# Low products shared out tile by tile, and two products placed later in their engines' orders, in a scan and expert kernel

## The chip, the cores and the metric

The kernel runs on one core of a Trainium2 chip. The time is the device time of one launch in microseconds (us). The kernel before took 1074.97 us, the median of 3 runs (1071.48 to 1076.53).

## What is computed

The input x has 2 rows of 1024 tokens of width 512. It is normalised per token (layernorm, called xn below). Two branches read xn, and their product is added to x.

```
proj = xn @ W_in.T ; x, gate = halves of proj (1024 each)
x  = silu(conv_b + causal 4-tap convolution of x along the tokens)
ts, Bm, Cm = rms-normalised parts of x @ W_x.T     (32, 16, 16)
dt = softplus(ts @ W_dt.T + b_dt)
state[d, n] = state[d, n] * exp(dt[d] * A[d, n]) + dt[d] * x[d] * Bm[n]   over the tokens
y[d] = sum over n of state[d, n] * Cm[n]
s  = ((y + x * D) * silu(gate)) @ W_out.T
g  = silu(top-2-of-8 expert mixture of xn)          (expert: 512 x 512)
out = x_in + s * g
```

Everything is float32. The recurrence is what makes the work serial: every one of 1024 channels with 16 states each needs a scan over 1024 tokens, twice.

## The kernel before, in words

**Tiles and quads.** The tokens are cut into 4 chunks c of 512 (chunks 0 and 1 are the first row, 2 and 3 the second), the 1024 channels into 8 tiles t of 128. n = 8c + t counts the 32 tiles, and all loops of the main part run over n. A tile's 16 states per channel are laid out as 4 quads q of 4 banks of [128 x 512]; m = 4n + q counts the 128 quads. Banks 0 and 1 of a quad are its low half, banks 2 and 3 its high half.

**One quad** takes these steps, each on its own engine: ScalarE makes the decays exp(dt*A) into PSUM (`decays`, L801); GpSimd makes the drives dt*x*B in a ring of 4 buffers in SBUF (`drives`, L588), from `rep`, which a DMA broadcasts out of DRAM for every tile; VectorE scans bank after bank (`scans`, L1175); the scanned states are multiplied by C, the high half always by VectorE (`products`, L1185), the low half either by VectorE or by GpSimd (`low_products`, L601); TensorE sums the product over the states into `y_ps` (`sums`, L1426). A drive buffer is free again when the sums of the quad 4 before are done. `POOL_QUADS` names for each tile the quads whose low product GpSimd makes; for these the low scans write to SBUF instead of PSUM. There are 98 of them.

**What ends a tile.** TensorE opens the sum of a tile with the skip product diag(D) times x (`skip`, L1420), which needs the tile before to have been read out of `y_ps`: VectorE multiplies `y_ps` by the silu of the gate (`gate_tile`, L1202), once the last quad of that tile is summed.

**Expert slots.** The tokens are sorted by expert into 23 slots of 128 rows for each of the two rows of input. Up to two slots are worked off in a tile, a first and a second one: TensorE transposes the slot (`turn_slot`, L1400), ScalarE copies the transposed slot to SBUF (`copy_slot_T`, L811), TensorE multiplies it by the expert's weights (`expert`, L1411), ScalarE copies the result out. GpSimd scatters token rows to the slots (`put_rows`, L552) and gathers them again (L566, L573).

**Around it.** In a tile, TensorE also makes the gate's products (`gate_in`, L1386), the x product of a tile of the next chunk (`next_x`, L1322, an early and a late one), the step sizes of two tiles on (L1363), and in tiles 8, 9, 16, 17, 18, 24 and 25 the output products of the chunk before (`out_tile`, L1458). ScalarE takes the first tap of the convolution (L710), VectorE the other three (`convolve`, L1114). VectorE makes step sizes out of the softplus parts (`step_sizes`, L1154 to L1150).

**What sets the order.** Every engine has its own instruction queue, written out by hand in one block per engine; an engine takes its instructions strictly in that order and waits at semaphores. Nothing is planned at run time. VectorE's order in tile n is: low scans and high half of quad 0, `gate_tile(n - 1)`, low half of quad 1, an early convolution, high half of quad 1, and so on. TensorE's order is: sums of the tile before's last quad, `gate_in`, `turn_slot` of the first slot, `skip`, at some tiles an output product, `expert` of the first slot, sums of quad 0, the late x product, the second slot. GpSimd's order in tile n is drives of quad 2, low product of quad 0, drives of quad 3, low product of quad 1, drives of the next tile's quad 0, low product of quad 2, drives of the next tile's quad 1, low product of quad 3, with row stores and gathers between.

Of the kernel before, what the change touches and what calls it, by code (L numbers as in the profile page):

```python
# [17 lines left out]
PER_ROW = SEQ // TC  # L18
# [21 lines left out]
ROWS = SLOTS * P  # L40
CONSTS = 2 * P + SLOTS + RT + P + BATCH * (E + 1)

POOL_QUADS = {n: (0, 1, 2) if 6 <= n < 14 else (0, 1, 2, 3) for n in range(TILES) if 2 <= n % (PER_ROW * NT) < 14}
POOL_QUADS.update({14: (2, 3), 15: (0, 1), 16: (3,), 17: (1, 2, 3), 30: (0, 3)})
SLOT_STEPS = ({2: (0, 1), 3: (2, 3), 4: (4, 5), 5: (6, 7), 6: (8, 9), 7: (10, 11), 8: (12, None), 9: (13, 14), 10: (15, 16), 11: (17, 18), 12: (19, 20), 13: (21, 22)},
              {2: (None, 0), 3: (1, 2), 4: (3, 4), 5: (5, 6), 6: (7, 8), 7: (9, 10), 8: (11, 12), 9: (13, 14), 10: (15, 16), 11: (17, 18), 12: (19, 20), 13: (21, 22)})
CLEARS = {n: (4 * (n - 1), min(4 * n, SLOTS)) for n in range(1, 7)}
# [54 lines left out]
def scan_moe(nc, x, wx_in, wg_in, wdt_in, wxp, wring, gate_w, means, a_log, conv_w, conv_b, d_skip,  # L102
             route_consts, bc_dram, rep_rows, xn_rows, xnT_rows, slot_x, slot_rows, s_rows, out):
    with ExitStack() as ctx:
# [877 lines left out]
        def _(dve):  # L982
# [196 lines left out]
            def products(m, h):  # L1179
                n, q = divmod(m, NQ)  # L1180
                c, t = divmod(n, NT)
                dve.wait_ge(scan_ok, NR * m + 2 * h + 2)
                if t == 0:
                    dve.wait_ge(s_c[q], 16 * (c + 1))
                dve.tensor_tensor(drive[:, m % RING, 2 * h:2 * h + 2, :], sc[:, 2 * h:2 * h + 2, :],  # L1185
                                  c_all[:, q:q + 1, :].broadcast_to([P, 2, TC]),
                                  ALU.mult).then_inc(high_ok if h else low_ok, 1)

            def low(m):
                scans(m, 0)  # L1190
                if not on_pool(m):
                    products(m, 0)
# [44 lines left out]
            for n in range(TILES):  # L1237
                c, t = divmod(n, NT)
                m = NQ * n
                early, late = early_x(c, t), late_x(c, t)  # L1240
                chunk_end = t == NT - 1 and c < NCH - 1
                rms_tile = t == NT - 2 and c < NCH - 1
                even = c % PER_ROW == 0
                after_odd = c and even
                if n:
                    low(m)
                    if pe_log(n + 1):
                        times_x(n + 1)
                    scans(m, 1)
                    if chunk_end and not pe_log(n + 1):  # L1250
                        step_sizes(n + 1)
                    products(m, 1)
                if n:
                    gate_tile(n - 1)
                low(m + 1)
                if early is not None:
                    convolve(NT * (c + 1) + early)
                scans(m + 1, 1)
                if after_odd and t == 2:
                    out_tile(c - 1, 3)  # L1260
                products(m + 1, 1)
                low(m + 2)
                if after_odd and t == 1:
                    out_tile(c - 1, 0)
                high(m + 2)
                if late is not None:
                    convolve(NT * (c + 1) + late)
                if after_odd and t == 1:
                    out_tile(c - 1, 1)
                low(m + 3)  # L1270
                high(m + 3)
                if rms_tile:
                    rms(c + 1)
                elif n + 2 < TILES and not pe_log(n + 2):
                    step_sizes(n + 2)
                if after_odd and t == 1:
                    out_tile(c - 1, 2)
# [8 lines left out]
        def _(pe):  # L1286
# [116 lines left out]
            def expert(b, j):  # L1403
                if j is None:
                    return
                m = SLOTS * b + j
                loads = ((SLOTS + 1) // 2 if j % 2 == 0 else SLOTS // 2) * b + j // 2 + 1
                pe.wait_ge(s_wr[j % 2], 16 * loads)
                pe.wait_ge(xt_ev, m + 1)
                for h in range(HK):  # L1410
                    last = pe.matmul(f_ps[:, :], xT_slot[:, h, :], w_ring[:, j % 2, h, :],  # L1411
                                     start=(h == 0), stop=(h == HK - 1))
                last.then_inc(f_mm, 1)

            def skip(n):
                c, t = divmod(n, NT)
                pe.wait_ge(diag_ok, n + 1)
                if n:
                    pe.wait_ge(gated, n)
                pe.matmul(y_ps[:, :], diag[:, :], xy[:, c % 2, t, :], start=True, stop=False).then_inc(skip_mm, 1)  # L1420

            def sums(m):
                low_done(pe, m)
                pe.wait_ge(high_ok, m + 1)
                for r in range(NR):
                    last = pe.matmul(y_ps[CH * r:CH * (r + 1), :], stack[:, :], drive[:, m % RING, r, :],  # L1426
                                     start=False, stop=(m % NQ == NQ - 1))
                last.then_inc(sum_ok, 1)
# [64 lines left out]
            for n in range(TILES):  # L1493
# [12 lines left out]
                if chunk_end:  # L1506
                    add_log(n + 1)
                turn_slot(b, first_slot)
                skip(n)
                if c and even and t == 2:  # L1510
                    out_tile(c - 1, 3, HK, NT)
                expert(b, first_slot)
                sums(m)
                if rms_tile:
                    pe.wait_ge(conv_ok, NT * (c + 2))
# [106 lines left out]
```

## Time and profile before

| | value |
|---|---|
| median of 3 runs | 1074.97 us |
| profiled execution, its own time | 1074.7 us |
| its span | 1072.9 us |
| VectorE (DVE) busy | 992.7 us, 93% |
| GpSimd (POOL) busy | 919.1 us, 86% |
| TensorE (PE) busy | 855.4 us, 80% |
| ScalarE (ACT) busy | 727.6 us, 68% |
| low and high products on VectorE (L1185) | 158 at 1224 ns |
| low products on GpSimd (L601) | 98 at 2415 ns |
| drives on GpSimd (L588) | 127 at 4604 ns |

An engine's busy time is a sum over its instructions; idle time counts only where the engine's next instruction was awaited by the chain that ends last. In a timeline, a row gives the start, the duration, the instruction's line and operands, how many were merged, and in brackets how long the engine was idle before and what ended that. A duration contains a fixed part that the next instruction of the engine can overlap, so the distance of two starts is the better price. DVE is VectorE, POOL GpSimd, PE TensorE, PEld its weight loads, ACT ScalarE, SP the engine that issues most DMAs.

### The profile page before, as it was taken

The page shows a single profiled execution, that of the slowest core. Times are in us where ns is not written, and L with a number is a line of the kernel's source. Part 1 is how long each engine was busy: PE and PEld are TensorE (multiplying, and loading weights), DVE is VectorE, ACT ScalarE, POOL GpSimd, SP SyncE. Part 2 cuts the span into 40 slices and gives each one's busy share as a digit, 9 for nine tenths or more (in the row PEclk, how much of TensorE's full clock was granted, in tenths as well). Part 3 has the DMA queues.
Part 4 walks back from the last instruction along what each step waited for, and adds up shares of the span by engine and source line. Part 5 has one row for each costly group of instructions (what it writes and reads, how often), then busy time and mean ns, then how long its engine had stood idle before and what let it go on. Part 6 is the DMA issues. An engine that isn't in the chain of part 4 may idle for free.

```text
span 1072.9 us, 10237 instructions
## 1 busy us (share of the span) xinstructions
PE 855.4 (80%) x2756; PEld 316.9 (30%) x2756; DVE 992.7 (93%) x1021; ACT 727.6 (68%) x1281; POOL 919.1 (86%) x326
## 2 busy tenths in 40 slices
PE   8944467899879998898756579889898999779467
PEld 5321122333323333333211123333332333223122
DVE  6779998999999989999999888899999889999977
ACT  3657666788877766778565566688778666667533
POOL 0626898989879998888798999899988998999997
PEclk9986678999989999999877869999999999889889
DMA  9857578767688576666743842965648556664726
GB/s 335 345 159 284 225 272 326 260 238 277 245 287 313 200 265 243 227 246 228 247 129 129 235 168 108 316 216 193 230 170 317 207 206 235 226 225 167 274 39 158
DMA packets 86585, 245.93 MB, mean 229 GB/s; under 512 B 9344, under 2 KB 10752, under 8 KB 79872
## 3 DMA queue, kind: packets, MB, share of 16 engines
q1 hardware_dynamic: 67712, 197.03, 51.4%
q10 hardware_dynamic: 12672, 31.46, 7.5%
q0 software_dynamic: 6144, 16.78, 5.8%
q8 instruction: 23, 0.38, 0.1%
q14 instruction: 34, 0.28, 0.1%
HBM read 183.11 MB, written 62.13 MB: 229 GB/s over the span
## 4 chain that ended last, share of the span: by engine, by line
DVE 35%; POOL 21%; PE 17%; issue 13%; DMA 7%; ACT 6%; SPq 2%; DVEq 0%; ACTq 0%; POOLq 0%
DVE sc_ps L1175 15%; POOL drive L588 12%; DVE drive L1175 8%; POOL drive L601 6%; PE x_ps L1458 5%; DVE x_ps L1114 3%; DVE drive L1185 3%; PE y_ps L1426 2%; PE f_ps L1411 2%; DMA rep<-rep_rows 2%; PE dt_ps L1386 2%; DMA rep_rows<-dtu 2%; PE x_ps L1322 1%; ACT sc_ps L801 1%; POOL moe L573 1%
## 5 line engine op out<-in xcount | busy, mean ns | idle before, releaser
L588 POOL TENSOR_TENSOR drive<-rep,b_all 128x2048 f32<-128x2048 f32 x127 | 581.6, 4604 | 49.5 <-DMA rep<-rep_rows 41.6
L801 ACT ACTIVATE sc_ps<-rep,a_neg 128x512 f32<-128x512 f32 x512 | 331.9, 681 | 93.2 <-DVE drive L1185 61.2
L601 POOL TENSOR_TENSOR drive<-drive,c_all 128x1024 f32<-128x1024 f32 x98 | 236.7, 2415 | 18.5 <-ACT state L780 14.1
L1426 PE MATMUL y_ps<-drive,stack 128*32 128x512 f32 x1024 | 153.9, 676 | 110.6 <-POOL drive L601 64.5
L1175 DVE TENSOR_TENSOR_SCAN sc_ps<-sc_ps,state,drive 128x512 f32<-128x512 f32 x160 | 196.1, 1271 | 5.5 <-POOL drive L588 4.2
L1185 DVE TENSOR_TENSOR drive<-sc_ps,c_all 128x1024 f32<-128x1024 f32 x158 | 193.4, 1224 | 5.3
L1175 DVE TENSOR_TENSOR_SCAN sc_ps<-sc_ps,drive 128x512 f32<-128x512 f32 x156 | 181.7, 1210 | 9.9 <-ACT sc_ps L801 5.9
L1411 PE MATMUL f_ps<-w_ring,xT_slot 128*128 128x512 f32 x368 | 171.3, 609 | 15.4 <-ACT xT_slot L811 15.4
L1386 PE MATMUL dt_ps<-xnT,w_g 128*128 128x512 f32 x232 | 121.1, 670 | 28.2 <-ACT dtu L768 28.2
L1175 DVE TENSOR_TENSOR_SCAN drive<-sc_ps,state,drive 128x512 f32<-128x512 f32 x96 | 117.6, 1266 | 3.2 <-ACT sc_ps L801 3.2
L1175 DVE TENSOR_TENSOR_SCAN drive<-sc_ps,drive 128x512 f32<-128x512 f32 x100 | 116.3, 1204 | 0.3 <-POOL drive L588 0.3
L1411 PEld LDWEIGHTS f_ps<-w_ring,xT_slot 128*128 128x128 f32 x368 | 68.2, 193 | 116.8 <-issue 116.3
L1322 PE MATMUL x_ps<-xnT,w_x 128*128 128x512 f32 x192 | 89.9, 611 | 3.8 <-DMA w_x<-wx_in 3.8
L1458 PE MATMUL x_ps<-w_out,xy 128*128 128x512 f32 x176 | 82.6, 615 | 0.0
L1426 PEld LDWEIGHTS y_ps<-drive,stack 128*32 128x32 f32 x1024 | 21.4, 113 | 202.6 <-issue 116.3
L1386 PEld LDWEIGHTS dt_ps<-xnT,w_g 128*128 128x128 f32 x232 | 47.3, 215 | 109.1 <-issue 109.1
L780 ACT ACTIVATE state<-sc_ps 128x2 f32<-128x2 f32 x78 | 13.1, 168 | 58.5 <-DVE drive L1185 58.0
L1322 PEld LDWEIGHTS x_ps<-xnT,w_x 128*128 128x128 f32 x192 | 35.6, 193 | 57.5 <-issue 52.0
L1458 PEld LDWEIGHTS x_ps<-w_out,xy 128*128 128x128 f32 x176 | 32.6, 194 | 50.8 <-issue 50.2
L1363 PE MATMUL dt_ps<-dt_in,w_dt 128*128 128x512 f32 x64 | 41.3, 731 | 6.8 <-DVE dt_in L1225 5.6
L1420 PE MATMUL y_ps<-xy,diag 128*128 128x512 f32 x64 | 34.1, 615 | 14.0 <-DVE xy L1202 14.0
L768 ACT COPY dtu<-dt_ps 128x512 f32<-128x512 f32 x32 | 18.7, 585 | 36.9 <-DVE dtu L1150 36.8
(187 smaller groups left out, 1048.1 us busy)
## 6 DMA issues: line engine op xcount, KB each, us to landing
rep<-rep_rows SPq DMA_DIRECT2D x128, 512.0 KB, 6.2
w_ring<-wring SPq DMA_DIRECT2D x46, 1024.0 KB, 5.6
rep_rows<-dtu ACTq DMA_DIRECT2D x32, 512.0 KB, 2.7
x_slot<-slot_x SPq DMA_DIRECT2D x46, 256.0 KB, 6.8
slot_rows<-y_slot ACTq DMA_DIRECT2D x46, 256.0 KB, 4.3
w_g<-wg_in SPq DMA_DIRECT2D x32, 256.0 KB, 7.6
w_x<-wx_in SPq DMA_DIRECT2D x24, 256.0 KB, 3.8
slot_x<-zeros SPq DMA_DIRECT2D x1, 5888.0 KB, 20.5
```

What stands on the lines that cost most here:

```text
L588: pool.tensor_tensor(drive[:, m % RING, :, :], rep[:, n % 2, :, 1, :], b_all[:, q:q + 1, :].broadcast_to([P, NR, TC]), ALU.mult).then_inc( ...
L601: pool.tensor_tensor(drive[:, m % RING, 0:2, :], drive[:, m % RING, 0:2, :], c_all[:, q:q + 1, :].broadcast_to([P, 2, TC]), ALU.mult).then ...
L801: act.activation(sc[:, r, :], rep[:, n % 2, r, 0, :], ACT.Exp, scale=a_neg[:, lo:lo + 1]).then_inc(decay_ok, 1)
L1175: dve.tensor_tensor_scan(to, sc[:, r, :], drive[:, m % RING, r, :], state[:, lo:lo + 1] if follows else 0.0, ALU.mult, ALU.add).then_inc(s ...
L1185: dve.tensor_tensor(drive[:, m % RING, 2 * h:2 * h + 2, :], sc[:, 2 * h:2 * h + 2, :], c_all[:, q:q + 1, :].broadcast_to([P, 2, TC]), ALU. ...
L1322: last = pe.matmul(x_bank(j), w(h), xnT[:, c % 2, h, :], start=(h == 0), stop=(h == HK - 1))
L1363: pe.matmul(dt_ps[:, :], w_dt[:, t, :], dt_in[:, :], start=True, stop=True).then_inc(dt_mm, 1)
L1386: mm = pe.matmul(gate_bank(c, t)[:, :], w_g[:, h, :], xnT[:, c % 2, h, :], start=(h == 0), stop=(h == HK - 1))
L1411: last = pe.matmul(f_ps[:, :], xT_slot[:, h, :], w_ring[:, j % 2, h, :], start=(h == 0), stop=(h == HK - 1))
L1420: pe.matmul(y_ps[:, :], diag[:, :], xy[:, c % 2, t, :], start=True, stop=False).then_inc(skip_mm, 1)
L1426: last = pe.matmul(y_ps[CH * r:CH * (r + 1), :], stack[:, :], drive[:, m % RING, r, :], start=False, stop=(m % NQ == NQ - 1))
L1458: last = pe.matmul(bank, xy[:, c % 2, t, P * i:P * (i + 1)], w_out[:, t, :], start=(t == 0), stop=(t == NT - 1))
```

## The change

Three edits. The table of GpSimd's quads is changed: tile 0 gets quads 1 and 2, tile 6 gets quad 3; quad 3 of tile 16, quads 1 to 3 of tile 17, and quad 3 of tiles 18, 24 and 30 go to VectorE. VectorE's gate product of the tile before comes behind the low half of quad 1 instead of ahead of it. TensorE's skip product comes behind the first slot's expert products (and behind the output product that stands there in tile 18) instead of ahead of them.

```diff
--- before.py
+++ after.py
@@ -40,8 +40,8 @@
 ROWS = SLOTS * P
 CONSTS = 2 * P + SLOTS + RT + P + BATCH * (E + 1)
 
-POOL_QUADS = {n: (0, 1, 2) if 6 <= n < 14 else (0, 1, 2, 3) for n in range(TILES) if 2 <= n % (PER_ROW * NT) < 14}
-POOL_QUADS.update({14: (2, 3), 15: (0, 1), 16: (3,), 17: (1, 2, 3), 30: (0, 3)})
+POOL_QUADS = {n: (0, 1, 2) if 7 <= n < 14 else (0, 1, 2, 3) for n in range(TILES) if 2 <= n % (PER_ROW * NT) < 14}
+POOL_QUADS.update({0: (1, 2), 14: (2, 3), 15: (0, 1), 18: (0, 1, 2), 24: (0, 1, 2), 30: (0,)})
 SLOT_STEPS = ({2: (0, 1), 3: (2, 3), 4: (4, 5), 5: (6, 7), 6: (8, 9), 7: (10, 11), 8: (12, None), 9: (13, 14), 10: (15, 16), 11: (17, 18), 12: (19, 20), 13: (21, 22)},
               {2: (None, 0), 3: (1, 2), 4: (3, 4), 5: (5, 6), 6: (7, 8), 7: (9, 10), 8: (11, 12), 9: (13, 14), 10: (15, 16), 11: (17, 18), 12: (19, 20), 13: (21, 22)})
 CLEARS = {n: (4 * (n - 1), min(4 * n, SLOTS)) for n in range(1, 7)}
@@ -1250,9 +1250,9 @@
                     if chunk_end and not pe_log(n + 1):
                         step_sizes(n + 1)
                     products(m, 1)
+                low(m + 1)
                 if n:
                     gate_tile(n - 1)
-                low(m + 1)
                 if early is not None:
                     convolve(NT * (c + 1) + early)
                 scans(m + 1, 1)
@@ -1506,10 +1506,10 @@
                 if chunk_end:
                     add_log(n + 1)
                 turn_slot(b, first_slot)
-                skip(n)
                 if c and even and t == 2:
                     out_tile(c - 1, 3, HK, NT)
                 expert(b, first_slot)
+                skip(n)
                 sums(m)
                 if rms_tile:
                     pe.wait_ge(conv_ok, NT * (c + 2))
```

## Rows read from the trace of the kernel before

**Rows 1.** The chain that ended last, shares of the span by engine.

```profile
DVE 35%; POOL 21%; PE 17%; issue 13%; DMA 7%; ACT 6%; SPq 2%; DVEq 0%; ACTq 0%; POOLq 0%
```

**Rows 2.** VectorE's waits: us in total, times, longest.

```profile
DVE xy L1202 <- PE y_ps L1426: 11.4, 7, 4.0
...
DVE drive L1175 <- ACT sc_ps L801: 3.2, 4, 0.9
```

**Rows 3.** VectorE's timeline, tile 6, from quad 2: start us, us, instruction.

```profile
282.30 2.33 DVE L1175 TENSOR_TENSOR_SCAN drive<-sc_ps,drive 128x512 f32<-128x512 f32 x2
...
288.04 2.33 DVE L1175 TENSOR_TENSOR_SCAN sc_ps<-sc_ps,drive 128x512 f32<-128x512 f32 x2
...
295.07 0.68 DVE L1219 SCALAR_TENSOR_TENSOR dt_ps<-dt_ps,t_w 64x512 f32<-64x512 f32 x1
```

**Rows 4.** Timelines of GpSimd and VectorE, tiles 0 and 1.

```profile
101.75 9.05 POOL L588 TENSOR_TENSOR drive<-rep,b_all 128x2048 f32<-128x2048 f32 x2 [8.72 <-DMA rep<-rep_rows]
...
130.67 4.53 POOL L588 TENSOR_TENSOR drive<-rep,b_all 128x2048 f32<-128x2048 f32 x1
...
135.23 2.35 DVE L1175 TENSOR_TENSOR_SCAN sc_ps<-sc_ps,drive 128x512 f32<-128x512 f32 x2 [0.81 <-POOL drive L588]
```

**Rows 5.** Timelines of tiles 4 and 5, and a stretch of tile 4.

```profile
216.55 5.37 PE L1411 MATMUL f_ps<-w_ring,xT_slot 128*128 128x512 f32 x8 [0.36 <-ACT xT_slot L811]
...
227.26 0.78 ACT L710 ACTIVATE x_ps<-x_pad,cb,cw 128x512 f32<-128x512 f32 x1
...
228.59 1.54 DVE L1114 SCALAR_TENSOR_TENSOR x_ps<-x_pad,cw,x_ps 128x512 f32<-128x512 f32 x2
...
245.59 0.60 PE L1400 MATMUL f_ps<-ident,x_slot 128*128 128x128 f32 x4
246.03 1.02 PE L1420 MATMUL y_ps<-xy,diag 128*128 128x512 f32 x2
246.96 3.67 PE L1411 MATMUL f_ps<-w_ring,xT_slot 128*128 128x512 f32 x8
...
255.97 0.78 ACT L710 ACTIVATE x_ps<-x_pad,cb,cw 128x512 f32<-128x512 f32 x1
...
257.22 1.54 DVE L1114 SCALAR_TENSOR_TENSOR x_ps<-x_pad,cw,x_ps 128x512 f32<-128x512 f32 x2
...
core 0: us, PE busy (x) PEld busy (x) DVE busy (x) ACT busy (x) POOL busy (x), PEclk, DMA share, GB/s
...
216.50:222.00 5.50, 5.45 (x12) 2.18 (x16) 5.39 (x7) 4.69 (x8) 3.90 (x2) 0.69 0.91 311
```

**Rows 6.** Timelines of GpSimd, TensorE and VectorE, tiles 7 to 10.

```profile
316.72 2.37 POOL L601 TENSOR_TENSOR drive<-drive,c_all 128x1024 f32<-128x1024 f32 x1 [2.28 <-ACT state L780]
...
351.09 1.07 PE L1426 MATMUL y_ps<-drive,stack 128*32 128x512 f32 x8 [1.24 <-POOL drive L601]
...
406.43 1.54 DVE L1114 SCALAR_TENSOR_TENSOR x_ps<-x_pad,cw,x_ps 128x512 f32<-128x512 f32 x2 [0.91 <-ACT x_ps L710]
```

**Rows 7.** TensorE, VectorE and a DMA (from the chain), tiles 17 to 19.

```profile
635.84 1.94 PE L1426 MATMUL y_ps<-drive,stack 128*32 128x512 f32 x8 [3.72 <-POOL drive L601]
...
646.15 0.69 DVE L1208 TENSOR_TENSOR moe<-x_ps,moe 128x512 f32<-128x512 f32 x1 [3.17 <-PE x_ps L1458]
...
671.40 6.65 DMA w_x<-wx_in
...
684.42 0.69 DVE L1202 TENSOR_TENSOR xy<-y_ps,gate 128x512 f32<-128x512 f32 x1 [4.04 <-PE y_ps L1426]
...
695.67 2.35 DVE L1175 TENSOR_TENSOR_SCAN sc_ps<-sc_ps,drive 128x512 f32<-128x512 f32 x2 [0.34 <-ACT sc_ps L801]
```

**Rows 8.** GpSimd's drives from 905.3 to 1028.9, then VectorE's timeline to the end.

```profile
L588 POOL TENSOR_TENSOR drive<-rep,b_all 128x2048 f32<-128x2048 f32 x18 | 82.3, 4610 | 4.3 <-DMA rep<-rep_rows 4.2
...
1028.86 2.47 DVE L1175 TENSOR_TENSOR_SCAN sc_ps<-sc_ps,state,drive 128x512 f32<-128x512 f32 x2 [4.17 <-POOL drive L588]
...
1037.62 0.69 DVE L1202 TENSOR_TENSOR xy<-y_ps,gate 128x512 f32<-128x512 f32 x1 [1.41 <-PE y_ps L1426]
...
1064.76 2.51 DVE L1214 TENSOR_TENSOR xy<-xy,xnT 128x512 f32<-128x512 f32 x1
```

## The prediction

> **What bounds the kernel now.** I read the page's chain of waits first, then VectorE's idle time by releaser, then the timelines of VectorE, GpSimd, TensorE and ScalarE from 78 us to the end. The chain [rows 1] has no single owner: VectorE holds most of it, GpSimd and TensorE a good deal. VectorE's own waits [rows 2] are small: the gate product waited for TensorE 11.4 us in 7 places, the most that its move can return. What matters is which of VectorE's waits ends each stretch, because all else there is shifted only with it. I follow one number through the kernel: how much later (+) or earlier (-) VectorE reaches a place than before. All sums are made on the profiled execution: span 1072.9 us, time 1074.7 us, 0.3 us under the median 1074.97.
>
> **The price of one product.** With the low product on GpSimd, VectorE steps from one quad to the next in 288.04 - 282.30 = 5.74 us; with its own in 295.07 - 288.04 = 7.03 us [rows 3]. So a product costs VectorE 1.3 us; it saves GpSimd 2.3 us, a little under the 2.37 us of the product in [rows 6], since the next instruction starts just before it ends. Counted from the table, GpSimd goes from 98 to 94 products. On a VectorE that never waited the four would cost 5.2 us; what they cost here depends on each place.
>
> **Tiles 0 and 1 (quads 1 and 2 to GpSimd): +2.3 us.** GpSimd waits 8.72 us for the broadcast before the drives at 101.75 [rows 4], so quad 1's product is free. Quad 2's comes after the first of these two drives and pushes everything behind it: the second drive, 16 indirect stores in three bundles, and drives up to quad 7's at 130.67. VectorE already waited 0.81 us for that one [rows 4]. VectorE and ScalarE arrive 1.3 us sooner, but the drive lands 2.3 us later, so quad 7's scans start 2.3 us later. Behind them hang tile 3's step sizes and, behind the last stores, the slot load for tile 2, so tile 2's stalls move too. Bounds: -1.3 (the delay hidden, the sooner arrival kept) and +2.3; the nearest row is the 0.81 us wait, which leaves no room, so I take +2.3.
>
> **The skip product behind the slot's products: a gap that nothing fills.** In tile 5, TensorE ends the slot's transposes at about 246.2, runs the skip product at 246.03 and starts the expert's products at 246.96 [rows 5]: the skip product fills the time in which ScalarE copies the transposed slot. Put last, it leaves that gap open and adds 0.85 us to TensorE's queue before the quad's sums. In most tiles TensorE has slack. It lacks it where the late x product follows: in tile 5 ScalarE starts its tap at 255.97 and is through 0.5 us before VectorE's convolution at 257.22, in tile 4 it starts at 227.26 for a convolution at 228.59, slack 0.6 us [rows 5]. TensorE runs without a pause from tile 4's second slot to tile 5's, so the second delay adds to the first: 1.85 us less 0.5 of slack gives +1.4 for the two. Bounds: 0 (cover found) and +2.0. The same sums in tiles 11 to 13 and 20 and 21 stay inside 0.35 to 2 us of slack: 0.
>
> **Tile 6 (quad 3 to GpSimd): -1.3 us.** GpSimd waits again behind it before tile 7's products (the 2.28 us in [rows 6] is the last of these waits), and VectorE's steps follow without waits, also through the normalisation. Bounds: -1.3 and 0.
>
> **Tiles 7 to 10: +1.1 us.** VectorE's waits end on a chain that leaves it in tile 7: keep-state copy, GpSimd at 316.72 with its 2.28 us wait, drives and products of tile 8, TensorE at 351.09, which then never pauses until tile 10's late x product, awaited by VectorE at 406.43 [rows 6]. The gate moved behind the second quad's low scans starts this chain 0.6 us sooner, tiles 9 and 10 each add 0.85 for the uncovered skip product. -0.6 + 1.7 = +1.1; bounds -0.6 and +2.0. The gate wait of 1.0 us in tile 10 gives nothing: behind it the scans wait for ScalarE, which waits for the same output product.
>
> **Tiles 16 to 19 (quad 3 of 16, three quads of 17 and quad 3 of 18 to VectorE): -1.9 us.** Five products, 6.5 us of VectorE and 11.5 us off GpSimd. VectorE's scans of tile 17 start where the drive lands, which none of this moves. Then TensorE no longer waits 3.72 us for GpSimd's product before its sums at 635.84; the output tile follows 2.4 us sooner, and VectorE, which waited for it 3.17 us until 646.15 [rows 7], passes 2.4 us sooner in spite of three more products. From there the chain is GpSimd's residual, the weight load that landed 6.65 us after 671.40, the x product, the sums and ScalarE's tables: -2.5 us. The 4.04 us gate wait at 684.42 [rows 7] vanishes almost wholly, but VectorE then waits for ScalarE, 0.34 us before and now for 2.5 us earlier work at 695.67. So of the gate's 4 us only the chain's 2.5 remain, and tile 19's uncovered skip product takes 0.65 back. Bounds: +6.5 (no cover at all) and -4.7 (VectorE before its next wait).
>
> **Tiles 23 to 30: +0.3 us.** The tile 7 pattern again: -0.6 for the gate, +0.85 for tile 25; quad 3 of tile 24 lies in a wait of VectorE for softplus. From the broadcast of tile 27 on GpSimd has no idle time: in the stretch to quad 124 its drives show 4.3 us, all before the first [rows 8]. None of the products in that stretch leaves GpSimd before the drive for which VectorE waited 4.17 us at 1028.86, so the +0.3 arrives there whole, and VectorE's shift before it does not count.
>
> **Tile 30 and the end: -2.3 us.** Quad 3's product is gone from GpSimd right behind that drive. The gate wait of 1.41 us at 1037.62 goes [rows 8]: -1.4. GpSimd's tail of sums is 2.3 us sooner, and VectorE's first closing sum, 2.51 us at 1064.76 where its like take 0.68 [rows 8], ended only as GpSimd fell idle. So the end gains the full 2.3; bounds -2.3 and 0. The Trainium skill, SBUF — State Buffer, section "Who interferes with whom", says that a VectorE product with both inputs in SBUF and a GpSimd one block each other for a whole instruction; by that rule the long row is a lock, and the gain at the end would be 2.3 rather than 1.4 us.
>
> **Sum.** +2.3 + 1.4 - 1.3 + 1.1 - 1.9 + 0.3 - 2.3 = -0.4 us: 1074.7 - 0.4 = 1074.3 us. The moves of work return some 5.5 us and give back 5.
>
> **Rivals.** *The skip product stays covered.* If TensorE's real slack is larger than the modelled ends show, 1.4 + 1.7 + 0.65 + 0.85 = 4.6 us go: 1069.7 us; with quad 2's delay hidden as well, 3.6 more: 1066.1. For it: TensorE is busy 80% and the copy takes only 0.6 us. Against it: four of VectorE's waits already sit behind a TensorE queue with no pause.
>
> *TensorE's clock falls in the new gap (the slower side).* In the tiles where TensorE waits for the gate, it has transposes, 1.6 us idle, skip product, 0.4 us idle, expert. After the change that is one pause of over 3 us. In tile 4 the expert's products took 5.37 us at a granted clock of 0.69 for that stretch, against 3.67 in the row of tile 5 [rows 5]: 1.7 us more each, on the queue that already lacks slack. It decides where a pause of 3 us lowers the clock from 2.4 to 1.2 GHz. In four such tiles it is +6.8: 1081.1 us. Against it: the sums behind are mostly awaited by nobody at once. The Trainium skill, TensorE: Matmul & The Clock Gate, Part 1 (the HAM clock gate), says that an idle array is put back to half rate and needs activity to be released; by that rule the new pause makes this rival likelier than rows alone do, and tile 4's row agrees.
>
> *The gate's move returns its waits whole.* 11.4 less the last tile's 1.3 is 10.1 us: 1064 us. Against it: in four places the scans behind have a wait of their own for ScalarE, 3.2 us in all [rows 2], and three of these follow a gate wait. So I give it little.
>
> **How the numbers follow.** Forecast 0.50, its own range 1071.5 to 1077. Covered skip product 0.27, clock 0.18, whole gate waits 0.05. About 0.5% (5.4 us) is what a measurement tells from no change: below 1069.6 is faster, above 1080.3 slower. Forecast: nearly all of it within 0.5%, 0.04 each side. First rival: some two thirds below 1069.6. Second: seven in ten above 1080.3. Third: faster. Together faster 0.27, same 0.57, slower 0.16. The range 1067 to 1080.5 leaves out the lower end of the first and third rivals and the upper of the second.
>
> **What would show it.** Right: VectorE's products L1185 at 162 and GpSimd's L601 at 94; quad 7's scans in tile 1 near 137.5 with a wait of about 4 us for GpSimd; the skip product starting right where the expert's products end, with 0.8 us idle between transposes and expert; new short waits of VectorE for ScalarE before the late convolutions of tiles 4 and 5; waits for the gate under 3 us in sum; the wait before quad 124 still for a drive, the last VectorE sums at 0.7 us. Wrong: tile 1's scans no later than before, tiles 4 and 5 without waits, or a fall of the granted clock in tiles 4, 6, 20 and 22.

## The result: half a per cent slower

The changed kernel took 1080.27 us (median of 6 runs, 1078.08 to 1081.23), the kernel before on the same chip 1074.2 us (6 runs). The ratio is 1.0049, with a 95% interval of 1.0032 to 1.0066: 5.3 us, about 0.5%, slower. I had forecast 1074.3 us and a change within 0.5% as the likeliest case. The time lies inside my range, close to its upper edge, but the change went the other way than the sum, which had it 0.4 us faster. The mechanism that came true was one of my rivals, to which I had given 0.18.

The profiled execution took 1080.09 us, span 1078.3 us. Its chain by engine, to be held against [rows 1]:

```profile
DVE 28%; PE 28%; POOL 20%; issue 10%; DMA 7%; ACT 4%; SPq 2%; DVEq 0%; POOLq 0%; ACTq 0%
```

TensorE's share of the chain has gone from 17% to 28%, though its busy time has not grown by anything near that. VectorE's waits after, in the form of [rows 2] (us in total, times, longest):

```profile
DVE sc_ps L1175 <- ACT sc_ps L801: 11.4, 10, 2.4
DVE sc_ps L1175 <- POOL drive L588: 9.5, 3, 4.4
...
DVE drive L1175 <- ACT sc_ps L801: 7.9, 3, 2.6
DVE x_ps L1114 <- ACT x_ps L710: 5.3, 8, 1.2
...
DVE xy L1202 <- PE y_ps L1426: 1.4, 1, 1.4
```

The waits for the gate, 11.4 us before, have all but gone, as intended. But waits for ScalarE stand in their place. Before, two of these rows were:

```profile
DVE sc_ps L1175 <- ACT sc_ps L801: 7.2, 8, 2.4
...
DVE x_ps L1114 <- ACT x_ps L710: 2.0, 2, 1.1
```

The wait ahead of the scans into `sc_ps` grew from 7.2 to 11.4 us, that ahead of the scans into `drive` from 3.2 to 7.9, and eight convolutions in place of two wait for their first tap. ScalarE in turn waits for TensorE. What TensorE waits for says why; the same view, first of before, then of after:

```profile
PE f_ps L1411 <- ACT xT_slot L811: 15.4, 21, 1.2
PE y_ps L1420 <- DVE xy L1202: 14.0, 10, 2.9
```

```profile
PE f_ps L1411 <- ACT xT_slot L811: 48.4, 34, 4.3
...
PE y_ps L1420 <- DVE xy L1202: 29.6, 6, 8.8
```

L1411 is the expert product of a slot. It waited 15.4 us for ScalarE's copy of the transposed slot, never over 1.2 us; now it waits 48.4 us, up to 4.3. Tile 6 shows one such wait. TensorE's timeline (start, us), before and then after:

```profile
272.34 0.60 PE L1400 MATMUL f_ps<-ident,x_slot 128*128 128x128 f32 x4
274.55 1.10 PE L1420 MATMUL y_ps<-xy,diag 128*128 128x512 f32 x2 [1.61 <-DVE xy L1202]
276.01 3.67 PE L1411 MATMUL f_ps<-w_ring,xT_slot 128*128 128x512 f32 x8 [0.36 <-ACT xT_slot L811]
```

```profile
274.83 0.60 PE L1400 MATMUL f_ps<-ident,x_slot 128*128 128x128 f32 x4
278.50 5.37 PE L1411 MATMUL f_ps<-w_ring,xT_slot 128*128 128x512 f32 x8 [3.07 <-ACT xT_slot L811]
283.70 1.02 PE L1420 MATMUL y_ps<-xy,diag 128*128 128x512 f32 x2
284.66 1.07 PE L1426 MATMUL y_ps<-drive,stack 128*32 128x512 f32 x8
```

Transposes to expert product: 276.01 - 272.34 = 3.67 us before, 278.50 - 274.83 = 3.67 us after. The expert product does not start a moment sooner for having left the skip product's company. It waits for the copy either way, and the skip product had been running inside that wait. Now it runs behind, and the pause in front of the expert product is unbroken. Here is what the pause does (windows: stretch, length, busy time of PE, PEld, DVE, ACT, POOL, granted clock, DMA share, GB/s), before and after:

```profile
276.00:279.70 3.70, 3.69 (x12) 1.51 (x16) 3.63 (x5) 2.95 (x5) 3.70 (x2) 1.00 0.91 275
```

```profile
275.40:278.50 3.10, 0.03 (x1) 0.03 (x1) 3.10 (x4) 2.56 (x6) 3.10 (x2) 1.00 0.87 318
278.50:283.80 5.30, 5.30 (x9) 2.28 (x10) 5.19 (x8) 5.14 (x8) 4.34 (x2) 0.68 0.84 298
```

Behind a stretch with TensorE idle the granted clock is 0.68 on average, between the levels of 1.2 and 2.4 GHz, and the same eight products take 5.37 us in place of 3.67. In tiles 7 and 23 the pause is 4.34 us and the products take 5.98 and 5.93 us. The price then reaches VectorE through the second slot's transposes and ScalarE's queue:

```profile
295.24 2.35 DVE L1175 TENSOR_TENSOR_SCAN sc_ps<-sc_ps,drive 128x512 f32<-128x512 f32 x2 [2.37 <-ACT sc_ps L801]
```

Why the copy is late can be read on ScalarE's own timeline:

```profile
273.08 1.30 ACT L801 ACTIVATE sc_ps<-rep,a_neg 128x512 f32<-128x512 f32 x2
274.32 0.19 ACT L705 ACTIVATE x_pad<-halo 128x3 f32<-128x3 f32 x1
274.42 0.56 ACT L707 COPY x_pad<-x_ps 128x512 f32<-128x512 f32 x1
275.07 0.78 ACT L710 ACTIVATE x_ps<-x_pad,cb,cw 128x512 f32<-128x512 f32 x1
275.79 0.19 ACT L712 ACTIVATE halo<-x_pad 128x3 f32<-128x3 f32 x1
276.34 0.17 ACT L780 ACTIVATE state<-sc_ps 128x2 f32<-128x2 f32 x1 [0.36 <-DVE drive L1185]
276.54 1.30 ACT L801 ACTIVATE sc_ps<-rep,a_neg 128x512 f32<-128x512 f32 x2
277.78 0.57 ACT L811 COPY xT_slot<-f_ps 128x512 f32<-128x512 f32 x1
```

The transposes end at 275.43, and in its written order ScalarE has the early x block and two decays to do before the copy. The copy is late like this in tiles 4, 6, 20 and 22, which have an early x (pause 3.07 us), and in tiles 7 and 23, the last of a chunk, where ScalarE first copies the next chunk's step sizes and waits 1.2 us for VectorE to make them (4.34 us). An early x is not enough: tiles 3, 5, 19 and 21 have one too, but their pause is 0.77 us; in tile 5 ScalarE is at the copy first and waits 1.22 us for the transposes.

### The profile page after: what moved, and what is told of

It is laid out like the page before. It is cut to its first block, busy times and chain, and to the rows that moved or that the text cites. A ratio compares the mean times of both kernels' runs of the same rounds, so it can differ in the third digit from the quotient of the medians.

```text
span 1078.3 us, 10234 instructions
## 1 busy us (share of the span) xinstructions
PE 860.6 (80%) x2756; PEld 323.2 (30%) x2756; DVE 997.3 (92%) x1025; ACT 727.0 (67%) x1281; POOL 909.9 (84%) x322
## 4 chain that ended last, share of the span: by engine, by line
DVE 28%; PE 28%; POOL 20%; issue 10%; DMA 7%; ACT 4%; SPq 2%; DVEq 0%; POOLq 0%; ACTq 0%
DVE sc_ps L1175 12%; POOL drive L588 11%; PE f_ps L1411 6%; DVE drive L1175 6%; PE x_ps L1458 5%; POOL drive L601 4%; PE y_ps L1426 4%; PE x_ps L1322 3%; PE dt_ps L1386 3%; DMA rep<-rep_rows 3%; DVE drive L1185 3%; DVE x_ps L1114 2%; DMA rep_rows<-dtu 2%; POOL moe L573 2%; PE x_ps L1344 1%
## 5 line engine op out<-in xcount | busy, mean ns | idle before, releaser
L601 POOL TENSOR_TENSOR drive<-drive,c_all 128x1024 f32<-128x1024 f32 x94 | 224.4, 2388 | 16.0 <-DVE sc_ps L1175 5.8
L1411 PE MATMUL f_ps<-w_ring,xT_slot 128*128 128x512 f32 x368 | 179.6, 634 | 48.4 <-ACT xT_slot L811 48.4
L1175 DVE TENSOR_TENSOR_SCAN sc_ps<-sc_ps,state,drive 128x512 f32<-128x512 f32 x164 | 201.2, 1272 | 4.9 <-POOL drive L588 3.1
L1185 DVE TENSOR_TENSOR drive<-sc_ps,c_all 128x1024 f32<-128x1024 f32 x162 | 198.4, 1224 | 5.4
L1175 DVE TENSOR_TENSOR_SCAN sc_ps<-sc_ps,drive 128x512 f32<-128x512 f32 x160 | 186.6, 1212 | 16.5 <-ACT sc_ps L801 9.5
L1175 DVE TENSOR_TENSOR_SCAN drive<-sc_ps,state,drive 128x512 f32<-128x512 f32 x92 | 112.7, 1266 | 7.9 <-ACT sc_ps L801 7.9
L1411 PEld LDWEIGHTS f_ps<-w_ring,xT_slot 128*128 128x128 f32 x368 | 71.4, 202 | 142.1 <-issue 141.2
L1175 DVE TENSOR_TENSOR_SCAN drive<-sc_ps,drive 128x512 f32<-128x512 f32 x96 | 111.7, 1205 | 0.0
L811 ACT COPY xT_slot<-f_ps 128x512 f32<-128x512 f32 x46 | 26.6, 579 | 33.5 <-PE f_ps L1400 33.5
L1114 DVE SCALAR_TENSOR_TENSOR x_ps<-x_pad,cw,x_ps 128x512 f32<-128x512 f32 x54 | 40.7, 753 | 6.5 <-ACT x_ps L710 5.3
```

The costliest lines, as they stand in the source:

```text
L601: pool.tensor_tensor(drive[:, m % RING, 0:2, :], drive[:, m % RING, 0:2, :], c_all[:, q:q + 1, :].broadcast_to([P, 2, TC]), ALU.mult).then ...
L1114: tap = dve.scalar_tensor_tensor(out=x_bank(j) if k < K - 1 else xy[:, c % 2, t, :], in0=padded(j)[:, k:k + TC], scalar=cw[:, t * K + k:t ...
L1175: dve.tensor_tensor_scan(to, sc[:, r, :], drive[:, m % RING, r, :], state[:, lo:lo + 1] if follows else 0.0, ALU.mult, ALU.add).then_inc(s ...
```

## The experiments

The change has three parts: the **table** of products, the **gate** product behind the second quad's low scans, and the **skip** product behind the first slot's products. Runs of one group shared a chip and the runs of the kernel before; ratios are to that kernel, with 95% intervals. Microseconds "by the ratio" are differences of ratios times 1074 us. In edits the names are those of the diff.

### All combinations of the three parts

**Table alone.** The edit leaves the new `POOL_QUADS` and takes the other two parts back.

```diff
-                low(m + 1)
                 if n:
                     gate_tile(n - 1)
+                low(m + 1)
...
+                skip(n)
                 if c and even and t == 2:
                     out_tile(c - 1, 3, HK, NT)
                 expert(b, first_slot)
-                skip(n)
```

> The kernel before with the new table of c products alone; gate product and skip product at their old places. Theory 1 (TensorE's queue): what the change lost came from the skip product leaving the gap in which TensorE waits for ScalarE's copy of the first slot (3.07 us idle in tiles 6, 18 and 22, 4.34 in tiles 7 and 23, with the slot's eight products at 5.37 to 5.98 us behind it in place of 3.67), so the table alone keeps the gain of tiles 16 to 20 (the shift after - before falls from 6.33 to 1.64 us there) and pays 1.2 us in tile 0: 1069 to 1073. Theory 2 (the table): the quads of tiles 0 and 6 and the ones given back late in the table are the loss: 1078 to 1081.

Measured: 1070.67 us, ratio 0.9982 (0.9966 to 0.9998). The table is a gain, 1.9 us by the ratio, just clear of nothing. Theory 2 falls. (Where the expectation says tile 18, the pause is that of tile 20.)

**Gate and skip without the table** (old `POOL_QUADS` in the changed kernel):

```diff
-POOL_QUADS.update({0: (1, 2), 14: (2, 3), 15: (0, 1), 18: (0, 1, 2), 24: (0, 1, 2), 30: (0,)})
+POOL_QUADS.update({14: (2, 3), 15: (0, 1), 16: (3,), 17: (1, 2, 3), 30: (0, 3)})
```

and 6 in place of 7 in the table's range.

> The changed kernel with the old table: only the gate product and the skip product stand at their new places. Theory 1 (TensorE's queue): slower than the changed kernel by what the table gives, 1081 to 1086, with about 3 us idle and a slow first slot in tiles 6, 7, 22 and 23 still there. Theory 2 (the table): 1070 to 1074.

Measured: 1080.79 us, 1.0075 (1.0053 to 1.0098), just below the range of theory 1. The first slot's pause of 3.07 us stands in tiles 4, 6, 20 and 22, that of 4.34 in 7 and 23.

**Table and gate, skip product at its old place:**

```diff
+                skip(n)
                 if c and even and t == 2:
                     out_tile(c - 1, 3, HK, NT)
                 expert(b, first_slot)
-                skip(n)
```

> The changed kernel with the skip product back ahead of the first slot's products; table and gate product as changed. The skip product then waits for a gate product that stands 2.3 us later on VectorE, and the slot's products stand behind it. Theory 1a (the pair belongs together: with the late gate product the old order is as bad): 1080 to 1085, the slot's products start behind the gate product in every tile. Theory 1b (the skip product's place alone is the loss): 1069 to 1073. Theory 2 (the table): 1078 to 1081.

Measured: 1081.31 us, 1.0068 (1.0046 to 1.0091). Theory 1a: the later gate product must not have the skip product, and the expert product behind it, waiting for it.

**Table and skip, gate product at its old place:**

```diff
-                low(m + 1)
                 if n:
                     gate_tile(n - 1)
+                low(m + 1)
```

> The changed kernel with the gate product back ahead of the second quad's low scans; table and skip product as changed. Theory 1 (the skip product's place is the loss, whenever the gate product comes): 1078 to 1082, with the 3 us gap and the slow first slot of tiles 6, 7, 22 and 23 as in the changed kernel, and VectorE's waits for sums ahead of the gate product back (some 11 us in sum, a part of them in place of other waits). Rival (the late gate product holds the sums back): 1069 to 1074.

Measured: 1081.74 us, 1.0069 (1.0050 to 1.0089). VectorE's gate waits are back at 10.6 us and the time is not better: with the skip product behind, the gate's place matters little.

**Skip product alone** (the last two lines of the diff on the kernel before):

```diff
-                skip(n)
                 if c and even and t == 2:
                     out_tile(c - 1, 3, HK, NT)
                 expert(b, first_slot)
+                skip(n)
```

> The kernel before with the skip product behind the first slot's products and nothing else changed. Theory 1 (its place is the loss with either gate order): 1079 to 1084. Rival (it loses only together with the new table or the late gate product): 1072 to 1076.

Measured: 1081.75 us, 1.0072 (1.0053 to 1.0091).

**Gate product alone:**

```diff
+                low(m + 1)
                 if n:
                     gate_tile(n - 1)
-                low(m + 1)
```

> The kernel before with VectorE's gate product behind the second quad's low scans, and nothing else changed: the skip product is ahead of the slot's products still. Theory 1 (the order of TensorE's queue decides: skip product, and with it the slot's products, wait for a gate product that is 2.3 us later): 1080 to 1085. Rival (the later gate product costs only together with the new table): 1072 to 1076.

Measured: 1085.32 us, 1.0102 (1.0081 to 1.0123), the slowest of all and just above what theory 1 gave. TensorE's timeline in tile 6 of this kernel, and its windows there:

```profile
273.99 0.60 PE L1400 MATMUL f_ps<-ident,x_slot 128*128 128x128 f32 x4
278.43 2.05 PE L1420 MATMUL y_ps<-xy,diag 128*128 128x512 f32 x2 [3.84 <-DVE xy L1202]
280.27 5.32 PE L1411 MATMUL f_ps<-w_ring,xT_slot 128*128 128x512 f32 x8
```

```profile
277.00:280.00 3.00, 1.57 (x2) 0.84 (x3) 2.93 (x5) 2.72 (x5) 3.00 (x2) 0.50 0.92 299
280.20:285.50 5.30, 5.30 (x9) 1.95 (x7) 5.26 (x6) 4.69 (x8) 1.63 (x1) 0.67 1.00 364
```

The pause is 3.84 us, the skip product in it runs at a granted clock of 0.50 and takes 2.05 us, the expert product 5.32. Slow products behind a long pause are there with the other order too, so they hang on the pause, not on which product comes first.

Together, as ratios to the kernel before:

```
                  old table            new table
neither           1                    0.9982
gate              1.0102               1.0068
skip              1.0072               1.0069
gate and skip     1.0075               1.0049
```

Each way of reordering costs. With the new table both together cost least by the number, but the intervals of the three overlap. The table by itself is the only part that gains. Beside the gate product it gains too, just measurably; beside both its 0.26% is within the noise, and beside the skip product there is nothing. The change is 0.67% slower than its own table alone, 7.2 us; from the two intervals this difference is good to about 2.5 us.

### Where the 7.2 us are

How much later VectorE reaches the product `dtu` (L1150) for tile k than in the kernel before, read off its timelines, us:

```
              k=3    k=8    k=12   k=18   k=21   k=24   k=31
table alone   1.8   -0.2    0.2    1.8   -2.4   -2.4   -2.8
changed       2.6    3.7    5.2    6.3    1.6    5.4    7.4
six tiles     1.9    0.2    2.2    3.6    0.3    1.9    4.0
gap filled    2.4    0.2    1.5    2.8   -0.4    0.4    0.6
```

Against the table alone the changed kernel loses 3.1 us between k = 3 and 8 (3.9 - 0.8) and 3.8 between 21 and 24 (7.8 - 4.0). VectorE does this product one or two tiles ahead, so these are tiles 2 to 6 and 20 to 22, where the late copies are; k = 24 to 31 adds 2.4 more. These are single executions, and their level is uncertain by more than tenths: the table without tile 0's quads, an experiment further down, leaves everything up to tile 5 as in the kernel before, and still reaches k = 4 2.0 us earlier. Steps inside a row tell more than the level of a row. The last two rows are the next two experiments.

**Old order in the six tiles with a late copy** (`LATE_COPY = (4, 6, 7, 20, 22, 23)`):

```diff
+                if n in LATE_COPY:
+                    gate_tile(n - 1)
                 low(m + 1)
-                if n:
+                if n and not n in LATE_COPY:
                     gate_tile(n - 1)
...
+                if n in LATE_COPY:
+                    skip(n)
                 expert(b, first_slot)
-                skip(n)
+                if not n in LATE_COPY:
+                    skip(n)
```

(the lines of the output tile between them stand as they were)

> The changed kernel with the old order (gate product ahead of the low scans, skip product ahead of the slot's products) in the six tiles where ScalarE's copy of the first slot comes 3.07 to 4.34 us after the transposes: 4, 6, 7, 20, 22 and 23. The loss by the order was 1080.3 - 1070.7 = 9.6 us. Theory 1a (it falls in these six tiles): 1071 to 1074, no gap over 2 us ahead of a first slot, none of its eight products slower than in the kernel before, and the new waits of 2.37 us of VectorE in tiles 6 and 22 gone. Theory 1b (it is spread: 0.8 us in every tile where TensorE is what VectorE ends up waiting for): 1077 to 1080.

Measured: 1075.43 us, 1.0013 (1.0000 to 1.0026). Between the two: 0.36% or 3.9 us of the 7.2 come back; the rest, by this run, lies in the other tiles. One expectation missed: in tiles 7 and 23 the products still took 5.76 and 5.72 us, behind a wait of 2.89 us (tile 7) for the gate.

**The gap filled.** The order stays as changed, but TensorE has work in the pause. Three parts of the gate's input product are computed once more with results thrown away, and the last three real parts come behind the transposes. Dependences and results stay, TensorE has 36 matmuls more:

```diff
+                if n in LATE_COPY:
+                    for h in range(HK - 1):
+                        gate_part(n, h, HK - 2)
+                    gate_part(n, 0)
+                else:
+                    for h in range(HK):
+                        gate_part(n, h)
...
                 turn_slot(b, first_slot)
+                if n in LATE_COPY:
+                    for h in range(1, HK):
+                        gate_part(n, h)
```

> The changed kernel; in the same six tiles TensorE computes three parts of the gate's input product once more (2.75 us of matmuls with results that are thrown away, ahead of the first part) and the last three parts behind the transposes, inside the 3.07 or 4.34 us gap. Order and all results stay; the array is busy in the gap. Theory 1c (the idle gap costs the clock: 5.37 to 5.98 us for the slot's eight products in place of 3.67): the products run 3.7 us, the end comes 2 to 5 us earlier, 1075 to 1078.5. Theory 1d (the order alone, the skip product's 0.95 us behind the slot): the products stay above 5 us or their speed doesn't matter, 1079.5 to 1081.5.

Measured: 1075.17 us, 1.0017 (1.0004 to 1.0030). TensorE's timeline of tile 6, and its windows in the pause and behind it:

```profile
273.04 0.60 PE L1411 MATMUL f_ps<-ident,x_slot 128*128 128x128 f32 x4
273.47 2.74 PE L1396 MATMUL dt_ps<-xnT,w_g 128*128 128x512 f32 x6
276.70 3.67 PE L1422 MATMUL f_ps<-w_ring,xT_slot 128*128 128x512 f32 x8 [0.49 <-ACT xT_slot L812]
```

```profile
273.60:276.70 3.10, 2.61 (x7) 0.85 (x6) 3.10 (x4) 2.57 (x6) 3.10 (x2) 1.00 0.85 289
276.70:280.30 3.60, 3.60 (x9) 1.69 (x10) 3.53 (x6) 3.45 (x6) 3.60 (x2) 1.00 0.88 278
```

The expert product starts 3.66 us after the transposes, as always, but it runs at a granted clock of 1.00, in 3.67 us. All first slots of the six tiles do. By adding useless work to the pause the kernel became 3.4 us faster by the ratios (5.1 by the medians), at the far end of what theory 1c expected. That is what the low clock behind these six pauses cost: about half of the 7.2 us, though the two intervals would allow 1 to 6 us. It is not all a cost of the change: in tile 4 the products took 5.37 us in the kernel before and with the table alone as well, and filling the pause sped them up too. VectorE's wait of 2.37 us in tile 6 fell to 0.68.

**The copy earlier.** ScalarE copies ahead of the second quad's high decays in the same tiles:

```diff
+                if n in LATE_COPY:
+                    copy_slot_T(b, first_slot)
                 decays(m + 1, 1)
-                copy_slot_T(b, first_slot)
+                if n not in LATE_COPY:
+                    copy_slot_T(b, first_slot)
```

> The changed kernel; ScalarE copies the first slot's transposes ahead of the second quad's high decays in tiles 4, 6, 7, 20, 22 and 23, where it idles 0.36 to 0.55 us at that place. Theory 1 (the late copy makes the gap): the gap falls from 3.07 to about 1.2 us, the products run at 3.67 us, the skip product and the sums behind come 3.5 us earlier in these tiles, and the end 3 to 7 us earlier: 1073.5 to 1077.5. Rival (the decays that now come 0.25 us later cost VectorE as much, or the end hangs on other tiles): 1079 to 1081.5.

Measured: 1074.56 us, 1.0001 (0.9987 to 1.0014): 5.2 us less than the change by the ratios. Inside, one place went otherwise than expected. In tile 6 the gate's input product took 5.40 us behind a wait of 2.12 us for GpSimd's product, so ScalarE, now standing at the copy, waited 3.93 us for the transposes with the decays queued behind it. In tiles 7 and 23 the pause only fell to 2.81 us and the expert product still took 5.37. The gain came from the other tiles.

### The table's own terms

**Tile 0's quads back on VectorE,** table alone otherwise:

```diff
-POOL_QUADS.update({0: (1, 2), 14: (2, 3), 15: (0, 1), 18: (0, 1, 2), 24: (0, 1, 2), 30: (0,)})
+POOL_QUADS.update({14: (2, 3), 15: (0, 1), 18: (0, 1, 2), 24: (0, 1, 2), 30: (0,)})
```

> The new table alone, with tile 0's second and third quad back on VectorE. With the table alone VectorE was 1.04 us later than in the kernel before from tile 2 on and 0.22 us earlier behind tile 6. If those quads cost what they did there and nothing swallows it: 1069 to 1070.3 against 1070.7 of the table alone. Rival (what they cost is swallowed further on, or they give POOL's queue a lead): 1070.5 to 1072.

Measured: 1069.56 us, 0.9967 (0.9954 to 0.9980): the fastest version here, 3.5 us better than the kernel before and 1.1 us by the medians better than with tile 0's quads. That was measured on another chip, and the intervals of the two ratios overlap by about half, so this last difference is not shown.

**New order in tiles 19 and 31 only,** new table: `n in (19, 31)` selects the new places, all else is as with the table alone.

```diff
-                if n:
+                if n not in (0, 19, 31):
                     gate_tile(n - 1)
                 low(m + 1)
+                if n in (19, 31):
+                    gate_tile(n - 1)
...
-                skip(n)
+                if n not in (0, 19, 31):
+                    skip(n)
                 expert(b, first_slot)
+                if n in (0, 19, 31):
+                    skip(n)
```

> The new table, with the new order of gate product and skip product only in tiles 19 and 31: there VectorE still waited 2.40 and 1.82 us for sums ahead of the gate product with the table alone, and ScalarE's copy isn't late. If the order helps where no late copy stands behind it: 1067 to 1070. Rival (those waits come back as waits for decays or at the end): 1070 to 1072.

Measured: 1070.58 us, 0.9980 (0.9966 to 0.9993), no better than the table alone. VectorE in tile 19, with the table alone and then with the new order:

```profile
682.00 0.69 DVE L1202 TENSOR_TENSOR xy<-y_ps,gate 128x512 f32<-128x512 f32 x1 [2.40 <-PE y_ps L1426]
...
693.24 2.35 DVE L1175 TENSOR_TENSOR_SCAN sc_ps<-sc_ps,drive 128x512 f32<-128x512 f32 x2 [0.33 <-ACT sc_ps L801]
```

```profile
681.91 0.69 DVE L1202 TENSOR_TENSOR xy<-y_ps,gate 128x512 f32<-128x512 f32 x1 [0.39 <-PE y_ps L1428]
...
693.15 2.35 DVE L1175 TENSOR_TENSOR_SCAN sc_ps<-sc_ps,drive 128x512 f32<-128x512 f32 x2 [2.56 <-ACT sc_ps L801]
```

The wait for the sums shrinks by 2.0 us and the next wait, for ScalarE, grows by 2.2; the scans start at the same time. This is the pattern of [rows 7]. It shows for this tile, and the growth of the waits for ScalarE makes it likely for the others, why 11.4 us of gate waits were worth so little.

## Why the prediction was wrong

**The step that failed** is the skip product's. I wrote that in most tiles TensorE has slack, and priced the move at +1.4 us in tiles 4 and 5, and 0.85 or 0.65 us in four more. I took tile 5, where the gap is 0.8 us, as the pattern of all: "0.8 us idle between transposes and expert". In six tiles it is 3 to 4.3 us, because the copy stands behind other work on ScalarE. The rows of before held it: in tile 6 they show 1.61 us idle, skip product, 0.36 us idle, and I knew their sum to be "one pause of over 3 us". I used it for the rival only and left it out of the sum. There the skip product stood at +4.6 us and the gate's move took 0.6 off twice, so that the new order cost +3.4 at most. Measured, the skip product's new place alone costs 0.72%, 7.7 us, and both moves beside the new table 7.2.

**The clock rival was right** in its mechanism and its price of 1.7 us a tile. That its time was so near, 1081.1 against 1080.27, was partly luck. Two details were off. In tile 4 the products took 5.37 us before and after, so nothing was lost there; tiles 7 and 23, which I hadn't named, were worse (before, the products took 3.67 us in tile 7 and 4.83 in tile 23). And the filled gap returned 3.4 of the 6.8 us: the sum came out about right because other costs, which I had denied, made up the other half. I argued against this rival that "the sums behind are mostly awaited by nobody at once". VectorE indeed hardly waits for those sums (1.4 us in all); what hung on them was TensorE's own queue, the second slot's transposes in it, and ScalarE, which has its decays behind the copy of them. The Trainium skill, TensorE: Matmul & The Clock Gate, Part 1 (the HAM clock gate), says that the default state is the throttled one and that activity releases it. The trace agrees in tile 6: 0.68 behind the pause, 1.00 with it filled; not every such pause brings it, as the last section shows. I cited that rule and still gave the rival 0.18; rule and tile 4's row pointed the same way.

**Tile 6's quad, -1.3 us:** right for the table alone (the shift falls by 1.29 us from k = 7 to 8). In the changed kernel the wait of 2.37 us at 295.24 ate it.

**Tiles 0 and 1, +2.3 us:** quad 7's scans came 2.58 us later, behind the predicted wait:

```profile
137.81 2.35 DVE L1175 TENSOR_TENSOR_SCAN sc_ps<-sc_ps,drive 128x512 f32<-128x512 f32 x2 [4.42 <-POOL drive L588]
```

But "tile 2's stalls move too" was half wrong. The stall of 2.45 us there shrank to 0.42, and 1.2 us remained from tile 2 on. The experiment without tile 0's quads puts the whole at 1.1 by the medians, not clear of noise.

**Tiles 4 and 5:** the two predicted waits ahead of the late convolutions are there, 0.26 and 0.61 us long. In all the shift grows by 1.3 us from k = 5 to 7, against my 1.4. But the step hangs on the clock, which I hadn't said. It is 1.30 us in the changed kernel and with the gate product back, where tile 4's products took 5.37 us, and 0.01 in four kernels that also have the skip product behind but did these products in 3.67 (skip alone, both with the old table, gap filled, copy earlier). At full clock the uncovered 0.85 us found cover here.

**Tiles 7 to 10, +1.1 us:** 1.5 us in the changed kernel (k = 8 to 12), with the wait ahead of tile 10's scans:

```profile
397.81 2.46 DVE L1175 TENSOR_TENSOR_SCAN drive<-sc_ps,state,drive 128x512 f32<-128x512 f32 x2 [2.63 <-ACT sc_ps L801]
```

Before, the gate wait and the scans' wait here were 1.00 and 0.94 us. So the gate's wait came back as one for ScalarE, and 0.7 us more: the uncovered skip product, as reckoned. The shift says the same: from k = 11 to 12 it grows by 0.86 or 0.87 us in all seven kernels that have the skip product behind in tile 10 (changed, six tiles, gap filled, copy earlier, gate product back, skip alone, both with the old table), and not in the two of the table alone (-0.49 and 0.00).

**Tiles 16 to 19, -1.9 us:** -3.6 in the changed kernel (k = 17 to 21), inside the bound of -4.7. The direction held, the size was too small.

**Tiles 23 to 30, +0.3 us:** wrong. Tile 22, in which I had no cost, took the shift from 2.9 (k = 23) to 5.4, and from there to quad 124's scans it grew by 2.2 more. With the gap filled it grows by 0.2 us from k = 24 to 31, where the changed kernel's grows by 2.0. The +0.85 for tile 25 is in both: the shift grows by 0.85 from k = 26 to 27. More than half of the difference is one place, the gate's input product in tile 28, here in the changed kernel and then with the gap filled:

```profile
926.98 5.80 PE L1386 MATMUL dt_ps<-xnT,w_g 128*128 128x512 f32 x8
```

```profile
921.31 4.67 PE L1396 MATMUL dt_ps<-xnT,w_g 128*128 128x512 f32 x8
```

The granted clock is 0.63 over the first and 0.79 over the second; at 1.00 these eight take 3.70 us. Behind it VectorE waits 1.05 us for ScalarE in the changed kernel and not at all with the gap filled. But this follows a pause of 5.7 us, for a product of GpSimd, that both have and nothing fills, and both moves with the old table show 4.65 us. So it is the clock again, in a pause that the change didn't make, and one execution doesn't tell whether the change or chance made it worse.

**The end, -2.3 us:** quad 124's scans were 7.57 us late and the span 5.4, so 2.2 us came back. The closing sum I expected to fall from 2.51 [rows 8] to 0.7:

```profile
1070.95 1.56 DVE L1214 TENSOR_TENSOR xy<-xy,xnT 128x512 f32<-128x512 f32 x1
```

It fell to 1.56, to 1.19 us with the table alone, and to 0.68 without tile 0's quads. GpSimd's last sums and this row, before and then without tile 0's quads:

```profile
1062.44 4.27 POOL L618 TENSOR_TENSOR moe<-moe,w_ring 128x512 f32<-128x512 f32 x3
1064.76 2.51 DVE L1214 TENSOR_TENSOR xy<-xy,xnT 128x512 f32<-128x512 f32 x1
```

```profile
1053.28 4.28 POOL L618 TENSOR_TENSOR moe<-moe,w_ring 128x512 f32<-128x512 f32 x3
1058.45 0.68 DVE L1214 TENSOR_TENSOR xy<-xy,xnT 128x512 f32<-128x512 f32 x1
```

Before, the row ends 0.56 us after GpSimd falls idle (1067.27 - 1066.71), and so it does in the changed kernel (0.55) and with the table alone (0.56); where it starts after GpSimd's end, it takes 0.68 us. This fits the lock that the Trainium skill describes in SBUF — State Buffer, "Who interferes with whom". So the mechanism of this term held, and only the lead that GpSimd had was too small to free the whole row.

**Not settled.** Of the 7.2 us that the two moves cost beside the table, the filled gap returns 3.4, a part of which the kernel before paid too. The rest comes in small steps in many tiles. In tiles 10 and 25 these steps are the uncovered skip product, 0.85 us each by the shifts; for the others no run took the cause out by itself.

## What to carry to other kernels

Before moving an instruction out of a wait, add up the idle time around it: an instruction inside a pause is free, and behind the pause it can cost its own time and may cost the clock for what follows. A wait that goes from one engine is a gain only if the next wait does not end on the same chain; the pair 2.40 and 0.33 us turned into 0.39 and 2.56 at no gain. And take a change of several parts apart: here one part was a gain hidden by two that lose. With tile 0's two quads left where they were it gives 1069.56 us, ratio 0.9967, faster than both kernels.

## What I had not expected of the hardware

The same pause does not always bring the same clock. With gate and skip moved and the old table, the 3.07 us pause of tile 4 was followed by products at full rate (3.67 us), that of tile 6 by 5.37 us:

```profile
215.51 3.67 PE L1411 MATMUL f_ps<-w_ring,xT_slot 128*128 128x512 f32 x8 [3.07 <-ACT xT_slot L811]
...
274.98 5.37 PE L1411 MATMUL f_ps<-w_ring,xT_slot 128*128 128x512 f32 x8 [3.07 <-ACT xT_slot L811]
```

It is not a matter of the tile either: with the gate product back, tile 4's products took 5.37 us behind this pause and tile 6's 3.67. One such place proves nothing; what tells is the count over the tiles.

And a matmul whose result nobody needs can make a kernel faster: 36 of them were worth 3.4 us here, because what follows a filled pause ran at a granted clock of 1.00 in place of 0.60 to 0.68.
